# Rows of groups 2 to 15 turned on VectorE instead of TensorE, and another order of the setup, in a two-layer kernel of random features and experts

## What is computed

```python
xn = (x - mean) / sqrt(var + 1e-5)                       # per token
# layer 1: random features, for xn and for the rows of input_weights
f(v) = exp(xis) * exp(v @ (xis[:, None] * proj).T - 0.5 * sum(v * v) * xis**2) / sqrt(512)
attn = f(xn) @ f(input_weights).T
# layer 2: 64 experts, 8 per token, at most 256 tokens each, and a shared expert
scores = sigmoid(xn @ router_w)        # best 4 of 8 groups of experts, then the best 8 experts
e_out  = (silu(d @ gate_w[e]) * (d @ up_w[e])) @ down_w[e]      # d: rows of xn sent to e
shared = (silu(xn @ shared_gate) * (xn @ shared_up)) @ shared_down
out = x + attn + sum of weighted e_out + shared
```

## Time and profile before

| | us |
|---|---|
| three runs, median | 1409.01 |
| three runs, lowest and highest | 1363.36, 1427.19 |
| the profiled execution | 1371.13 |
| its span, first to last instruction | 1369.4 |
| mean granted TensorE clock | 0.990 of full speed |

### The profile page before, as it was taken

One profiled execution on the slowest core, in us unless ns is written; L12 is line 12 of the kernel. 1 busy time (PEld: TensorE's weight loads), 2 busy tenths in 40 slices (PEclk: granted clock), 3 DMA queues, 4 the chain that ended last, 5 costly groups with the idle time before them and its releaser, 6 DMA issues.

```text
span 1369.4 us, 22484 instructions
## 1 busy us (share of the span) xinstructions
PE 1322.0 (97%) x7837; PEld 1154.0 (84%) x7837; DVE 860.6 (63%) x1661; ACT 636.8 (47%) x988; POOL 480.6 (35%) x347
## 2 busy tenths in 40 slices
PE   6899999999999999999999999999999999999994
PEld 5688888888888888888888999999989999899983
DVE  7865656666566665657535666766666766676651
ACT  5311322123221232212325777677777777677762
POOL 1200000000000000000003677677767777676743
PEclk9899999999999999999999999999999999999997
DMA  6351333213332233312225999999999999999994
GB/s 209 133 192 52 108 129 128 87 63 107 128 128 68 81 107 128 128 53 96 78 76 162 276 284 283 286 282 280 290 275 284 292 287 291 276 297 285 280 248 62
DMA packets 166653, 250.00 MB, mean 183 GB/s; under 512 B 31450, under 2 KB 100318, under 8 KB 166622
## 3 DMA queue, kind: packets, MB, share of 16 engines
q1 hardware_dynamic: 137950, 178.28, 39.5%
q0 software_dynamic: 28672, 71.32, 22.6%
HBM read 178.18 MB, written 71.39 MB: 182 GB/s over the span
## 4 chain that ended last, share of the span: by engine, by line
PE 61%; DMA 22%; POOL 7%; issue 5%; DVE 2%; SPq 2%; ACT 1%; POOLq 0%; DVEq 0%
DMA out_dram<-outs,slot_cols 21%; PE pmm L1034 11%; PE pmm L1036 11%; PE pmm L1035 11%; PE pout L1034 7%; PE pout L1036 7%; PE pout L1035 7%; POOL out_dram L1383 6%; PE plog L1095 2%; PE ptr L1046 2%; POOL xbuf L1373 1%; PE ptr L1249 1%; SPq L339 1%; PE plog L1104 1%; DMA xbuf<-rows,slot_cols 1%
## 5 line engine op out<-in xcount | busy, mean ns | idle before, releaser
L1383 POOL DMA_INDIRECT out_dram<-outs,slot_cols x128 | 243.5, 1902 | 145.5 <-DMA out_dram<-outs,slot_cols 116.4
L1034 PE MATMUL pmm<-xt_hi,proj_hi 128*128 128x256 f32 (+1 forms) x784 | 252.7, 322 | 5.5 <-DVE xt_lo L989 2.4
L1034 PE MATMUL pmm<-xt_hi,sgu_hi 128*128 128x256 f32 (+1 forms) x768 | 251.8, 328 | 1.5 <-DVE hid L997 1.4
L1036 PE MATMUL pmm<-xt_hi,proj_lo 128*128 128x256 f32 (+1 forms) x784 | 249.3, 318 | 0.0
L1035 PE MATMUL pmm<-xt_lo,proj_hi 128*128 128x256 f32 (+1 forms) x784 | 249.3, 318 | 0.0
L1036 PE MATMUL pmm<-xt_hi,sgu_lo 128*128 128x256 f32 (+1 forms) x768 | 245.1, 319 | 0.0
L1035 PE MATMUL pmm<-xt_lo,sgu_hi 128*128 128x256 f32 (+1 forms) x768 | 244.7, 319 | 0.0
L1367 POOL TENSOR_TENSOR earlier<-earlier,chosen 128x64 bf16<-128x64 bf16 x64 | 28.6, 447 | 612.2 <-DVE chosen L759 608.4
L1373 POOL DMA_INDIRECT xbuf<-rows,slot_cols x128 | 195.1, 1524 | 90.6 <-DVE slot_cols L802 38.1
L473 ACT ACTIVATE feat<-pmm,ab 128x512 f32<-128x512 f32 x68 | 46.7, 687 | 317.2 <-PE pmm L1036 309.1
L1034 PEld LDWEIGHTS pmm<-xt_hi,proj_hi 128*128 128x128 f32 x784 | 147.4, 188 | 17.5 <-DVE xt_lo L989 2.8
(11 more groups left out here) (180 smaller groups left out, 2439.8 us busy)
## 6 DMA issues: line engine op xcount, KB each, us to landing
raw<-in_L_ffn_gate_w_dram SPq DMA_DIRECT2D x64, 512.0 KB
raw<-in_L_ffn_up_w_dram SPq DMA_DIRECT2D x64, 512.0 KB
raw<-in_L_ffn_down_w_dram SPq DMA_DIRECT2D x64, 512.0 KB
xbuf<-in_L_attn_x_dram SPq DMA_DIRECT2D x16, 1024.0 KB, 6.6
rows<-xn SPq DMA_DIRECT2D x16, 1024.0 KB, 4.2
outs<-in_L_attn_x_dram SPq DMA_DIRECT2D x32, 512.0 KB, 3.7
out_dram<-outs SPq DMA_DIRECT2D x32, 512.0 KB, 2.9
rows<-weight SPq DMA_DIRECT2D x16, 128.0 KB, 2.8
```

The costliest lines, as they stand in the source:

```text
L1034: pe.matmul(psum, lh, rh, start=first and n == 0, stop=False)
L1036: ins = pe.matmul(psum, ll, rh, start=False, stop=final and n == len(pairs) - 1)
L1383: pool.indirect_dma_start(out=out, out_offset=bass.IndirectOffsetOnAxis(ap=slot_cols[:, at:at + 1], axis=0), in_=outs[e.b][:, c, :], in_of ...
```

## The change

Groups 2 to 15 are no longer turned on PE. Their x is loaded so that partition p holds tokens whose number leaves the right remainder (`load_x_quads`, four DMAs), `normalise` writes xn with its columns ordered by blocks of 128, four DMAs copy it inside SBUF so that each block of columns lies on 32 partitions (`load_quad`, into `raw[1]`), and two DVE instructions transpose 32 x 32 squares into `raw[0]` (`turn_quad`). ACT copies the high part from there and DVE subtracts (`hi_quad`, `lo_quad`). xn is stored to `rows` from the quads, in runs of 127 or 128 elements, and its first column, which the norm now takes, is kept apart (`xn_first`) and stored in runs of one element (`store_xn_quads`). Features are taken in the order 4p + c, so that `load_rows` needs one DMA per matrix and the transposes that stay on PE read every fourth column.

deviations and normalise of group g+2 now stand at the end of group g, moments(g+2) ahead of scores(g+1). In the setup, router's low part comes ahead of features_lo 1, normalise(1) ahead of the shared weights, which are made in two halves on DVE, ACT and POOL; choose and weigh of group 0 follow hidden 0. The weights of experts 0 and 1 are loaded in group 14.

```diff
+        xn_quarters = xn[:].rearrange("p j h -> p (j h)").rearrange("p (b j c) -> p b j c", b=HB, j=J)
+        quad = raw[1][:, 0:J * H]
+        quad_blocks = quad.rearrange("p (k i c) -> p c k i", i=SQ, c=HB)
+        xt_whole = raw[0][:, 0:HB * GROUP].rearrange("p (c t) -> p c t", c=HB)
...
+            def load_x_quads(g):
+
+                for q in range(P // SQ):
+                    sp.dma_start(xbuf[g.b][q:P:P // SQ], x_quads[g.n, q]).then_inc(x_loaded[g.b], 16)
...
+            def load_rows(place, source, loaded):
+
+                sp.dma_start(place, source.rearrange("(p c) n -> p c n", p=P)).then_inc(loaded, 16)
...
+            def load_quad(g):
+
+                sp.wait_ge(norm_made, g.n + 1)
+                for b in range(HB):
+                    sp.dma_start(quad[b * SQ:(b + 1) * SQ, :], xn_quarters[:, b]).then_inc(quad_loaded, 16)
+
+            def store_xn_quads(g):
+                sp.wait_ge(quad_loaded, 16 * HB * (g.n - 1))
+                for b in range(HB):
+                    at = slice(1 if b == 0 else 0, P)
+                    sp.dma_start(rows_squares[g.n][:, :, b * P + at.start:(b + 1) * P],
+                                 quad[b * SQ:(b + 1) * SQ, :].rearrange("p (k c) -> p k c", c=P)[:, :, at]).then_inc(
+                        xn_stored, 16)
+                for q in range(P // SQ):
+                    sp.dma_start(rows_quads[g.n, q][:, :, 0:1], xn_first[q:P:P // SQ].unsqueeze(2),
+                                 allow_slow_non_contiguous=True).then_inc(xn_stored, 16)
...
+            def group(g, first=False):
+                nxt, later = g.next(), Turn(g.i + 1, g.b)
+                if first:
+                    store_xn(nxt)
+                else:
+                    load_x_quads(later)
                 load_residual(g)
-                if load:
-                    load_x(Turn(g.i + 1, g.b))
-                if not last:
-                    store_xn(g.next())
                 store_out(g, 0)
-                if not last:
-                    store_w(g.next())
-                    store_counts(g.next())
+                store_w(nxt)
+                store_counts(nxt)
+                load_quad(later)
+                store_out(g, 1)
+                store_xn_quads(later)
+
+            def before_last_group(g):
+                nxt = g.next()
+                load_residual(g)
+                sp.wait_ge(xn_stored, XN_STD + XN_QUAD * (GROUPS - 2))
+                sp.wait_ge(quad_turned, 2 * (GROUPS - 2))
+                load_gate_up(1, gate_w[1], up_w[1])
+                load_down(1, down_w[1])
+                sp.wait_ge(xt_lo_made, 2 * (GROUPS + 2))
+                load_gate_up(0, gate_w[0], up_w[0])
+                load_down(0, down_w[0])
+                store_out(g, 0)
+                store_w(nxt)
+                store_counts(nxt)
                 store_out(g, 1)
 
...
+            sp.dma_start(iw_raw[:, :, H:], iw.rearrange("(c p) d -> p c d", p=P)[:, :, 0:1],
+                         allow_slow_non_contiguous=True).then_inc(iw_loaded[1], 16)
             load_x(turn(0))
...
+            load_rows(shared_raw[:, 0], sgate_w, shared_loaded)
+            load_rows(shared_raw[:, 1], sup_w, shared_loaded)
...
+            load_x_quads(turn(2))
...
+            def hi_quad(g, half):
+
+                act.wait_ge(quad_turned, 2 * (g.n - 2) + half + 1)
+                act.wait_ge(up_done, IB * (g.n - 1))
+                at = slice(2 * half, 2 * half + 2)
+                act.activation(xt_hi[g.b][:, at, :], xt_whole[:, at, :], copy).then_inc(xt_hi_made, 1)
+
...
-            def group(g, last=False):
+            def group(g, first=False, last=False):
                 nxt = g.next()
-                for r in range(HB):
-                    features(1 + g.n, r, feat_hi)
-                if not last:
+                features(1 + g.n, 0, feat_hi)
+                features(1 + g.n, 1, feat_hi)
+                if first:
+                    for m in range(2):
+                        at = slice(m * GU // 2, (m + 1) * GU // 2)
+                        act.wait_ge(shared_less_made, m + 1)
+                        act.activation(sgu_hi[:, at], raw[0][:, at], copy).then_inc(shared_hi_made, 1)
+                features(1 + g.n, 2, feat_hi)
+                if not first and not last:
+                    hi_quad(nxt, 0)
+                features(1 + g.n, 3, feat_hi)
+                if not first and not last:
+                    hi_quad(nxt, 1)
+                if first:
+                    act.wait_ge(dn_loaded[0], 16)
+                    act.activation(sdn_hi[:], raw[0][:, GU:], copy).then_inc(shared_hi_made, 1)
...
                     xt_lo_made, 1)
 
+            def turn_quad(g, half):
+
+                dve.wait_ge(quad_loaded, 16 * HB * (g.n - 1))
+                at_least(dve, xt_hi_made, 2 * (g.n - 1 + 2) + 2)
+                at = slice(2 * half, 2 * half + 2)
+                dve.transpose(xt_whole[:, at, :].rearrange("p c (k i) -> p c k i", i=SQ),
+                              quad_blocks[:, at]).then_inc(quad_turned, 1)
+
+            def lo_quad(g, half):
+                dve.wait_ge(xt_hi_made, 2 * (g.n + 2) + half + 1)
+                at = slice(2 * half, 2 * half + 2)
+                dve.tensor_tensor(xt_lo[g.b][:, at, :], xt_whole[:, at, :], xt_hi[g.b][:, at, :].bitcast(F32),
...
 
-                dve.wait_ge(turned, 2 * (g.n + 2))
-                at_least(dve, xn_stored, 16 * g.n)
+                if isinstance(g.n, int) and g.n <= 2:
+                    dve.wait_ge(turned, 2 * (g.n + 2))
+                    at_least(dve, xn_stored, 32 * g.n)
+                else:
+                    dve.wait_ge(quad_loaded, 16 * HB * (g.n - 2))
+                    dve.wait_ge(xn_stored, XN_STD + XN_QUAD * (g.n - 2))
+                std = isinstance(g.n, int) and g.n < 2
+                first = xn[:, :, 0] if std else xn_quarters[:, 0, :, 0]
                 for j in range(J):
-                    ins = dve.tensor_scalar(xn[:, j, 0:H], xbuf[g.b][:, j, :], mean_var[:, j, 0:1],
-                                            rstd[:, j:j + 1], ALU.subtract, ALU.mult)
+                    if std:
+                        ins = dve.tensor_scalar(xn[:, j], xbuf[g.b][:, j, :], mean_var[:, j, 0:1], rstd[:, j:j + 1],
+                                                ALU.subtract, ALU.mult)
+                    else:
+                        ins = dve.tensor_scalar(xn_quarters[:, :, j], xbuf[g.b][:, j, :].rearrange(
+                            "p (b c) -> p b c", b=HB), mean_var[:, j, 0:1], rstd[:, j:j + 1], ALU.subtract, ALU.mult)
                 ins.then_inc(xn_made, 1)
                 step(dve.tensor_tensor(rstd2[:], rstd[:], rstd[:], ALU.mult), base)
-                dve.scalar_tensor_tensor(out=xn[:, :, H], in0=mean_var[:, :, 1], scalar=float(H),
-                                         in1=rstd2[:], op0=ALU.mult, op1=ALU.mult).then_inc(norm_made, 1)
+                dve.wait_ge(xn_made, g.n + 1)
+                dve.tensor_copy(xn_first[:], first).then_inc(first_kept, 1)
+                dve.wait_ge(first_kept, g.n + 1)
+                dve.scalar_tensor_tensor(out=first, in0=mean_var[:, :, 1], scalar=float(H), in1=rstd2[:],
+                                         op0=ALU.mult, op1=ALU.mult).then_inc(norm_made, 1)
 
...
                 features_lo(1 + g.n, 0, feat_hi, feat_lo)
                 if not last:
-                    deviations(nxt, base)
+                    turn_quad(nxt, 0)
                 features_lo(1 + g.n, 1, feat_hi, feat_lo)
                 if not last:
-                    normalise(nxt, base)
+                    turn_quad(nxt, 1)
                 features_lo(1 + g.n, 2, feat_hi, feat_lo)
+                if not last:
+                    lo_quad(nxt, 0)
                 features_lo(1 + g.n, 3, feat_hi, feat_lo)
                 if last:
                     pass_blocks(0)
                 else:
-                    lo_half(nxt.n + 2, 0, xt_hi[nxt.b], xt_lo[nxt.b])
-                    lo_half(nxt.n + 2, 1, xt_hi[nxt.b], xt_lo[nxt.b])
+                    lo_quad(nxt, 1)
                 hidden(g, 0, base)
                 hidden_lo(g, 0)
+                if not last and not before_last:
+                    moments(Turn(g.i + 1, g.b))
                 outputs(g, base, before_last, last)
 
             def outputs(g, base, before_last=False, last=False):
...
+            def finish(g, base, before_last=False, last=False):
+
+                nxt, later = g.next(), Turn(g.i + 1, g.b)
                 output(g, 0)
                 output(g, 1)
...
                 elif not before_last:
-                    moments(Turn(g.i + 1, g.b))
+                    deviations(later, base)
+                    normalise(later, base)
                 output(g, 2)
...
             features_lo(0, 3, wt_hi, wt_lo, scale=ab2[:, 3:4])
-            moments(turn(1))
             deviations(turn(1), 0)
+            normalise(turn(1), 0)
```

(43 more changed lines are left out.)

112 lines of the change are left out of this document (53 added, 59 removed).

## The result

| | before | after |
|---|---|---|
| median, us | 1375.68 (20 runs) | 1406.75 (20 runs) |
| lowest and highest | 1358.95, 1427.19 | 1388.27, 1462.42 |
| span of the profiled execution | 1369.4 | 1403.6 |

The ratio is 1.024, with a 95% interval of 1.0195 to 1.0282: the changed kernel is slower. Some executions of either kernel take over 1.5% longer than its fastest, and every ratio here leaves them out on both sides. The prediction said 1365 us, with 0.14 for slower, and its range ended at 1405.

A forecast was written before the change was run, and what follows sets the result against it. PE was taken to bound the kernel, busy 97% of the span. -27.4 + 3.5 - 0.9 = -24.8 made 1371.1 into 1346.3 us; half way from there to 1383.5, the same share off the median, gave 1365, range 1330 to 1405.

The forecast's parts named there:

- Transposes taken from PE: In the groups, 14 of them lose PE's transposes of the next rows, 1.96 us each: -27.4 us.
- moments: Moved on DVE to between hidden_lo(0) and scores; 0.25 us a group comes onto PE: +3.5 us.
- Where x stands in SP's queue: x, loaded behind the stores of xn, lands at 14.5 to 17, wanted at 18.8: hidden by 2 to 4 us.
- The ring: In the groups, x for the next statistics queues on SP behind copies and stores of xn: hidden, cost nothing.
- rival 1: In the groups, x comes late as 2560 short runs hold SP's queue: 1394 us, to 1411; chance 0.17.
- the copies: Four copies inside SBUF after normalise, which ends at -2.0: quad is in at about +2.6, late end +5.2.
- from the copies to x: Stores of xn, 160 runs per engine at 42 ns, take 6.7 us; x lands at about 14.5 to 17.
- The price of rival 1: In the groups, each microsecond that x lands past 18.8 costs 14 us.
- DVE's turns: Two transposes a group on VectorE, 1.1 us each, between 1.09 and 4.3; decides at about 3.4 us.
- The setup, net -0.9: Setup up to logits(1) 4.3 us earlier, then group 0 pays 3.4: net -0.9 us, between +3 and -6.
- The stall for DVE's work: In group 0, DVE's 17.6 us between hidden_lo(0) and output(0) make PE's attention(2) wait: +3.4 us.
- End of the groups: Weights of experts 0 and 1, loaded in group 14 behind the last stores, arrive in time: nothing.

The follow-up runs named there:

- x_ahead: The changed kernel with x's four loads issued behind the copies and ahead of the stores of xn: 1341.93 us, ratio 0.980 to the kernel before.
- turns_on_pe: The changed kernel with groups 2 to 15 turned on PE again and loaded and stored as before: 1373.4 us, ratio 1.0034 to the kernel before.
- firsts_behind: The changed kernel with x's loads between the quads' stores and the one-element stores: 1335.52 us, later 1348.5 us, ratio 0.9832 to the kernel before.
- copies_straight: The changed kernel with the four copies writing 128 partitions instead of 32, data then wrong: 1385.03 us in one run, period 41.2 us.
- firsts_quarter: The changed kernel with four added DMAs of 32 one-element runs each ahead of x: 1433.98 us in one run, period 49.3 us.
- firsts_one_more: The changed kernel with 512 added one-element runs in one DMA ahead of x: 1453.39 us in one run, period 47.1 us.
- turn_flat: x_ahead with DVE's turn reading consecutive elements instead of every fourth, data then wrong: 1388.92 us in one run, turn 1239 ns.
- residual_first: firsts_behind with xn(1) stored and group 0's residual loaded ahead of group 0's weights and counts: 1368.9 us, later 1344.9 us, ratio 0.9811 to the kernel before.

## Why the prediction failed, by its steps

- **Transposes taken from PE, -27.4.** Right. x_ahead has a period of 41.35 us; 43.25 - 1.96 = 41.29. With `moments` (0.19 measured in turns_on_pe, 0.06 here, 0.25 forecast) this is the sum of the group stage. The experts start at 711.65 in x_ahead, where the sum gives 735.2 - 24.8 = 710.4; that these agree so well is in part chance: x_ahead's setup lost 3.3 us (see the setup below), and firsts_behind, whose setup didn't, starts them at 707.62.
- **Where x stands in SP's queue.** This is the step that failed. The ring was seen, as rival 1, but the forecast put its cost at nothing, because its pieces were mis-sized. The working gave from the norm to x at the latest 19.0 us (17 - (-2.0)) with 20.8 wanted. It took 25.2 in the turn shown (226.96 to 252.14), 4.4 late, and 23.9 in the mean of eleven, 3.1 late. Both terms were low:
  - *the copies.* From the norm until they had landed 4.6 to 7.2 us were allowed; 10.1 were measured. The late end had doubled the transfer for 32 partitions. copies_straight shows 4.65 us with 128 partitions, which is the early end, so only having 32 on one side costs 5.4. The earlier trace rows couldn't show it, as no transfer there has so few partitions on a side. The Trainium skill (SBUF — State Buffer, Door 1: the DMA port swizzle) has half the rate for 32 partitions; this case's trace goes the same way and further: the whole, issue included, took 2.2 times as long, and the DMA engines moved 164 GB/s where they moved 377.
  - *from the copies to x.* 11.9 us were given: 6.7 for the 160 runs on each engine at 42 ns, the rest for the first packet and for x. It was 15.0 in this turn (237.09 to 252.14) and 13.8 in the mean. The price of the long runs was not the error: the packets of the 128 of them on each engine flow for some 5 us, near 40 ns each. What was left out is that SP issues twelve DMAs here, four of them x itself, at 0.7 to 1.0 us each: 2.84 + 4.10 + 3.10 = 10.0 us and the gaps between. The four one-element stores alone take 4.7 of it (240.10 to 244.82), while 32 runs at 42 ns would be 1.3: these 3.4 us cover the excess of 3.1. firsts_quarter against firsts_one_more shows that it goes by the number of DMAs. The prediction gave issues a price only for the copies (0.43 from the earlier trace rows; 0.65 measured).
  In the mean the copies were 2.9 us over their late end and the way to x 1.9 us over; the first is the larger, and either remedy alone (copies_straight, firsts_behind) ends the loss.
- **The price of rival 1.** It was put at 14 us for each microsecond late, which was too low. x was 3.15 us late in twelve groups, and it cost 12 x 4.45 = 53.4 us, 17 for each microsecond; by the prediction's price it would have been 14 x 3.15 = 44. Missing were the 1.4 us at the lower clock behind each wait; too many were two of the fourteen groups. So it is partly luck that its 1411 for 4.6 us late lies near the 1405.3 of the profiled execution (1403.6 + 1.7): the lateness was less and its price more. With the turns' -27.4, 0.8 for `moments` and 3.7 for the setup (below), 53.4 makes 30.5 of the 32.3 us lost before the experts. Its chance, 0.17, was too low. It had 2 to 4 us of slack against two terms without a row.
- **DVE's turns.** 1.1 us taken, 2.02 measured, inside the bounds (1.09 to 4.3) and under the 3.4 where it decides; hidden, as turn_flat shows. The prediction drew on the Trainium skill (Vector Engine (DVE) Microarchitecture Reference, The reshape front-end and per-opcode configuration) for one element per cycle and lane. The trace agrees roughly for consecutive reads, 1.24 us against 1.09 for two one-input passes over 512; in the kernel itself, with a step of 16 bytes, the measurement is 0.8 us more, and the measurement decides.
- **The setup, net -0.9.** The net is about right by offsetting errors. turns_on_pe has the first exponential of logits(2) at 113.98 us, before at 114.45, with the same transposes on PE: -0.5. But logits(1) came at 56.72 and not at 61 to 64, 10.2 us earlier than 66.92, and group 0 then lost 9.7. PE and ACT in turns_on_pe, then ACT before:
```profile
56.72 0.40 PE L1193 MATMUL plog<-xt_hi,router 128*128 128x512 f32 x1
```
```profile
113.98 0.38 ACT L543 ACTIVATE expn<-plog 128x256 f32<-128x256 f32 x1 [1.60 <-PE plog L1202]
```
```profile
114.45 0.38 ACT L496 ACTIVATE expn<-plog 128x256 f32<-128x256 f32 x1 [1.60 <-PE plog L1104]
```
  Group 0's waits are 4.4 for `outs` and 2.1 for the router's comparisons (`plog` for ACT's `beats`), and the rest is PE at the lower clock behind them: 0.94 of the clock over 57.26 us, 3.4 us. The stall for DVE's work was forecast at the right place, at 3.4 us where residual_first leaves 2.1; the residual that SP issued only at 74.17 (78.53 in after), behind `store_counts`, was overlooked, and so was ACT's `beats`. In after itself the setup did worse: logits(1) came at 59.60, and the first exponential of logits(2) at 116.19, where a transpose of 1.96 us is already gone; that is 116.19 + 1.96 - 114.45 = 3.7 us lost. x_ahead has 115.76, 3.3 us lost. The last section shows where 2.8 us of after's come from.
- **End of the groups.** Nothing, as forecast: no wait for the weights of expert 0 or 1 is among PE's waits in x_ahead, and the experts begin within 1.3 us of the sum.

## To carry to other kernels

When work is moved from the bounding engine to transfers, draw the ring that the new transfers close (here norm, copies, stores, x, moments, norm) and add up its pieces; the group can't be shorter than that, however idle each engine on it is. Count the DMAs that one engine issues in it, not only their bytes and runs, and let a load for the next step stand ahead of stores that nobody waits for: x_ahead takes the same change from 1.024 to 0.980 by where one call stands. Where the slack is 2 to 4 us and two of its terms have no row, the chance of missing it isn't a sixth.
